# Loading the adjacency of a graph layer in whole 128-partition transfers, from the SP and ScalarE queues

## The reference

```python
# layer 1, on h = layernorm(x)
mask = (adj > 0).astype(x.dtype)             # adj: 4096 x 4096 int32, 64 MiB
deg  = jnp.sum(mask, axis=1, keepdims=True)
agg  = mask @ h / jnp.maximum(deg, 1.0)
self_f, nb_f = h @ W_self + b_self, agg @ W_nb + b_nb
x = x + relu(concatenate([self_f, nb_f], -1) @ W_comb + b_comb)
# layer 2, on h = layernorm(x)
logits = h @ Wg + bg                         # 8 experts
score, idx = top_k(logits, 2); w = softmax(score)
x = x + sum over the two chosen e of w_e * (gelu(h @ W1[e] + b1[e]) @ W2[e] + b2[e])
```

## Time and profile before

| | |
|---|---|
| median of three runs | 504.6 us (504.56 to 507.19) |
| the profiled execution's own time | 503.99 us |
| its span, first to last instruction | 502.2 us |
| busy: PE, DVE, ACT, POOL | 435.5, 374.2, 261.2, 328.7 us |
| mean granted TensorE clock | 0.951 of full speed |
| moved by DMA | 122.48 MB, mean 244 GB/s |

### The profile page before, as it was taken

The page is one execution under the profiler, slowest core; times in us unless marked ns, Lnnn a source line. Parts: engine busy times, 40 slices in busy tenths (PEclk is TensorE's granted clock), DMA queues, the critical chain, the costliest instruction groups (busy, mean ns, idle before and its releaser), DMA issues.

```text
span 502.2 us, 12812 instructions
## 1 busy us (share of the span) xinstructions
PE 435.5 (87%) x4214; PEld 383.2 (76%) x4214; DVE 374.2 (75%) x1056; ACT 261.2 (52%) x403; POOL 328.7 (65%) x348
## 2 busy tenths in 40 slices
PE   5789999799999979999969998954999999997720
PEld 5578888688888868888848887843799999986610
DVE  2899654467779879797758788766677777779972
ACT  2566773144533534445435454233588888886630
POOL 3398585264665878877738876367777868665560
PEclk9999999999999989999979999995899999999975
DMA  8998799889995999799999997296865565598675
GB/s 216 272 292 251 210 228 284 234 236 279 279 279 159 294 280 281 209 292 302 299 295 267 297 310 228 87 286 214 264 194 175 176 178 178 169 337 339 198 220 167
DMA packets 48688, 122.48 MB, mean 244 GB/s; under 512 B 10601, under 2 KB 19693, under 8 KB 47600
## 3 DMA queue, kind: packets, MB, share of 16 engines
q1 hardware_dynamic: 26736, 64.09, 45.0%
q0 software_dynamic: 16144, 50.49, 33.5%
q10 hardware_dynamic: 5744, 7.08, 5.1%
HBM read 96.52 MB, written 26.93 MB: 246 GB/s over the span
## 4 chain that ended last, share of the span: by engine, by line
DVE 32%; PE 31%; DMA 14%; issue 9%; POOL 8%; ACT 3%; SPq 1%; DVEq 1%; ACTq 0%; POOLq 0%
PE bank L1342 8%; PE bank L1362 8%; DMA wst<-in_L_ffn_W_dram 8%; PE bank L1245 7%; DVE maskT L845 5%; POOL rs L633 3%; PE bank L1329 3%; DVE x_sb L930 2%; DVE xh L928 2%; DMA x_sb<-in_x_dram 2%; DVE w L982 2%; DMA stage<-in_adj_dram 2%; DVE st L934 2%; PE bank L1236 2%; ACT xh L725 2%
## 5 line engine op out<-in xcount | busy, mean ns | idle before, releaser
L1236 PE MATMUL bank<-z_flat,maskT 128*128 128x257 f16 x1024 | 231.3, 277 | 7.7 <-issue 7.6
L1237 PE MATMUL bank<-z_lo,maskT 128*128 128x256 f16 x1024 | 231.2, 276 | 0.0
L1236 PEld LDWEIGHTS bank<-z_flat,maskT 128*128 128x128 fp8e4 x1024 | 101.5, 99 | 21.6 <-issue 8.2
L651 POOL DMA_INDIRECT pair_out<-rows,enum x78 | 87.6, 1123 | 39.5 <-issue 18.3
L1237 PEld LDWEIGHTS bank<-z_lo,maskT 128*128 128x128 fp8e4 x1024 | 101.4, 99 | 12.8
L676 ACT ACTIVATE mask<-stage,m 128x2048 fp8e4<-128x2048 int32 x32 | 64.1, 2002 | 53.4 <-DMA stage<-in_adj_dram,gidx 39.7
L584 POOL DMA_INDIRECT dispatched<-rows,slot x64 | 66.4, 1038 | 28.0 <-issue 18.5
L573 POOL DMA_INDIRECT stage<-in_adj_dram,gidx x64 | 67.5, 1054 | 24.9 <-issue 13.3
L725 ACT ACTIVATE xh<-x_sb,nb,rs 128x256 f32<-128x256 f32 x32 | 19.2, 600 | 102.6 <-POOL nb L635 80.4
L633 POOL TENSOR_TENSOR rs<-ve,mhalf 128x1 f32<-128x1 f32 x32 | 39.8, 1245 | 49.4 <-DVE ve L939 49.1
L1342 PE MATMUL bank<-stage,w 128*128 128x256 f16 x468 | 59.7, 279 | 5.6 <-DVE stage L1115 5.3
(11 more groups left out here) (179 smaller groups left out, 604.9 us busy)
## 6 DMA issues: line engine op xcount, KB each, us to landing
stage<-in_adj_dram SPq DMA_DIRECT2D x256, 128.0 KB
stage<-dispatched SPq DMA_DIRECT2D x39, 260.0 KB, 3.0
wst<-in_L_ffn_W_dram ACTq DMA_DIRECT2D x16, 256.0 KB, 10.2
z_lo<-pair_out SPq DMA_DIRECT2D x4, 1024.0 KB, 7.1
dispatched<-pad SPq DMA_DIRECT2D x15, 260.0 KB
out_dram<-x_sb SPq DMA_DIRECT2D x28, 128.0 KB, 4.8
maskT<-pair_out SPq DMA_DIRECT2D x3, 1024.0 KB, 9.6
x_sb<-in_x_dram ACTq DMA_DIRECT2D x6, 256.0 KB, 11.4
```

The costliest lines, as they stand in the source:

```text
L651: gp.indirect_dma_start(out=yp_dram[:, :], out_offset=bass.IndirectOffsetOnAxis(ap=enum[:, a, s:s + 1], axis=0), in_=ysb[:, a, s, :], in_o ...
L1236: mm(acc[u % 2][:, 0:D + 1], a, z_hi[:, i, :], start=(i == 0), stop=False)
L1237: last = mm(acc[u % 2][:, 0:D], a, z_lo[:, i, :], start=False, stop=(i == NT - 1))
```

## The change

The view `adj_q`, the index column `gidx` with its semaphore and the function `gather` go, and with them all of GpSimd's 64 indirect DMAs on the adjacency. SP loads VectorE's half with one transfer for each b, over all 128 partitions, with g and r both taken whole from `adj_v`. For steps 0 and 1 SP loads ScalarE's half too. From step 2 on, ScalarE's own queue issues its half of step t+2 directly behind the mask of step t, after a wait for that mask's semaphore. The semaphore count of VectorE's half falls from 128 to 32 for each fill.

```diff
-    adj_q = adj.rearrange("n (g j) -> (n g) j", g=G)
@@ load_adj on SP
                 for b in range(2):
-                    for g in (0, 2, 1, 3):
-                        sp.dma_start(stage[Q * g:Q * g + Q, s, b, :], adj_v[t // B, t % B, g, :, b, :]).then_inc(s_adj[s], 16)
+                    sp.dma_start(stage[:, s, b, :], adj_v[t // B, t % B, :, :, b, :]).then_inc(s_adj[s], 16)
+                if t < 2:
+                    for b in range(2):
+                        sp.dma_start(stage[:, s + 1, b, :], adj_v[t // B, t % B, :, :, 2 + b, :]).then_inc(s_adj[s + 1], 16)
@@ GpSimd
-            pool.wait_ge(s_pad, 2)
-            for g in range(G):
-                if g:
-                    pool.wait_ge(s_gi, g)
-                gp.iota(gidx[Q * g:Q * g + Q, :], [[0, 1]], base=g, channel_multiplier=4 * B).then_inc(s_gi, 1)
-            pool.wait_ge(s_gi, G)
-            def gather(t):
...
-                if k == 1:
-                    gather(0)
...
-                if k in (2, 4, 5, 7):
-                    gather((2, 4, 5, 7).index(k) + 1)
-            gather(5)
...
-                m = made_in(s)
-                if m is not None and m + 2 < NT:
-                    gather(m + 2)
@@ masks on ScalarE
                 sc.activation(mask[:, u % 2, 2:4, :], stage[:, s], ACT.Sigmoid, bias=m100[:, 0:1], scale=200.0,
                               saturate=False).then_inc(s_mA, 1)
+                if t + 2 < NT:
+                    act.wait_ge(s_mA, t + 1)
+                    for b in range(2):
+                        act.dma_start(stage[:, s, b, :], adj_v[(t + 2) // B, (t + 2) % B, :, :, 2 + b, :]).then_inc(s_adj[s], 16)
@@ masks on VectorE
-                dve.wait_ge(s_adj[s], 128 * (div(t, u, known, 0, 2) + 1))
+                dve.wait_ge(s_adj[s], 32 * (div(t, u, known, 0, 2) + 1))
```

More of the change, by code:

```diff
@@ L114, in gnn_moe_kernel @@
         bcol = sb("bcol", [P, 2, KT], F32)
-        gidx = sb("gidx", [P, 1], I32)
         mhalf = sb("mhalf", [P, B], F32)
@@ L271, in gnn_moe_kernel @@
             "weights_transposed", "wT_copied", "weights_folded", "fold_hi", "fold_scales"))
-        s_gi = sem("gather_indices")
         s_fmx, s_fmr, s_fch, s_wf, s_bb, s_cp, s_cb = (sem(n) for n in (
@@ L614, in _ @@
                         normalise(t)
-                if k in (2, 4, 5, 7):
-                    gather((2, 4, 5, 7).index(k) + 1)
-            gather(5)
             pool.dma_start(b1c[:, :, :], b1.rearrange("e (t p) -> p e t", p=P), allow_slow_non_contiguous=True).then_inc(s_b12, 16)
-            self_and_const(0)
-            gather(6)
-            self_and_const(1)
+            for k in range(2):
+                self_and_const(k)
             LAST_POWERS = NT + X1
```

## The result

The changed kernel takes 904.33 us (median of four runs, 901.41 to 904.65) beside 505.25 us for the kernel before on the same chip: a ratio of 1.787, with an interval of 1.781 to 1.793. The forecast was 915 us. The profiled execution took 901.41 us, its span is 899.2 us.

A forecast was written before the change was run, and what follows sets the result against it. Transfers and TensorE were taken as close bounds before; after the change, four DMA engines. Adjacency 663, other traffic 52, start 2, tail 188 and 2 around the span sum to 907 us; some 8 for gaps gives 915, range 860 to 1130.

The forecast's parts named there:

- The layout: Adjacency transfers: source's outermost count of 4 puts both queues on the same 4 engines, not 16; chance 0.84.
- The rate of one engine: Adjacency transfers: each of four engines moves 25.3 GB/s, not 17.6, so 16.78 MB takes 663 us.
- The rest of the traffic and the gaps: Other transfers on the same engines 52 us, 2 us before them, some 8 us for gaps at the start.
- the queues stay full: Neighbour sum: each engine keeps its queue full, a step taking 21 us plus its share of the rest.
- Behind the last landing: After the last adjacency transfer: 3.2 us, 14.4 us of matmuls at half clock, 170.1 us to the end, together 188 us.
- Cover of ScalarE's issues: ScalarE's queue: 60 issues at 0.465 us, 0.93 us a step, 28 us in all, hidden and taken as 0.
- 300 each: Sign of being right: VectorE's and ScalarE's masks wait for the adjacency for 300 us and more each.
- the 40 us I allowed: Expert weights queue behind up to two steps of ScalarE's half, some 40 us, and just fit.
- GpSimd: Neighbour sum: 64 gathers, 67.5 us busy, go; worth between 0 and 14.6 us if transfers keep pace.
- My rival: Adjacency transfers spread over 16 engines after all, GpSimd's relief gives 0 to 14.6 us: 490 to 504 us; chance 0.12.
- Partition span and number of engines: Adjacency transfers: the 128-partition rule alone would make the change a gain; the outermost-count rule gives 4 engines.

The follow-up runs named there:

- e1: The changed kernel with the source's two outer indices exchanged (r, 32, outermost, then g), so another adjacency is summed: 508.87 us, 0.975 of the kernel before.
- e2: The changed kernel with each adjacency transfer cut into two of 64 partitions, 256 KB each: 1562.48 us, run once.
- e4: The kernel before with only SP's half in whole 128-partition transfers, the gathers kept: 709.97 us, 1.359 of the kernel before.
- e9: The same kernel as e1, run again beside e8 on one chip: 488.6 us, 0.970 of the kernel before.
- e3: The changed kernel with each transfer as four quarters of 32 partitions, 128 KB, on both queues, no gathers: 546.24 us, 1.042 of the kernel before.
- e5: As e3, quarters of 32 partitions on both queues, but both b in one transfer of 256 KB: 523.48 us, 1.036 of the kernel before.
- e8: The kernel before with b = 1 moved from SP's quarters to a third GpSimd gather over 128 partitions: 510.78 us, 1.014 of the kernel before.
- e6: The kernel before with SP's half in quarters of 256 KB, both b in one transfer, gathers kept: 509.0 us, 1.008 of the kernel before.

## Why the prediction was right, point by point

**The layout.** Right, and shown. Four engines carry the adjacency of both queues: 104 GB/s at a share of 0.26 with four packets in flight, e1 with only the index order changed at 0.975, e2 at half the rate with half the count, e4 with one queue alone at the same 104 GB/s.

**The rate of one engine.** I took 25.3 GB/s, from a stretch of long 128-partition loads, over the 17.6 of the sum. Measured: 26.0, on four engines and on two. The adjacency alone is then 16.78 MB / 26.0 = 645 us where I had 663. The choice of 25.3 was an argument, that sixteen engines share a limit which four don't reach, and at 17.6 the forecast would have been 1197 us; e2, with half as many engines and the same 26.0 for each, bears the argument out.

**The rest of the traffic and the gaps.** The last transfer lands at 708.3 us, where I had 663 + 52 + 2 and some 8 for gaps, 725. With 645 us for the adjacency 63 us are left for the rest, the start and any gaps, against my 62. That the queues stay full was right: between 25 and 700 us at least four packets are in flight for over 99% of the time. ScalarE made its 6th mask at 145.05 us and its last at 708.34: 563.3 us for 26 steps, 21.7 us each, where I had 21 us plus its share of the rest.

**Behind the last landing.** 899.2 - 708.3 = 190.9 us, forecast 188, with the right size by two errors. I let one step of matmuls follow, at half clock, 3.2 + 14.4 us. There are two, at nearly full clock: the matmuls of L1213 end at about 730.0, 21.7 us after the landing. ScalarE has the last mask, which waits for the landing, in its order ahead of the normalisation of an earlier tile (L701, L704). VectorE's subtraction L891 waits for that, and TensorE's transposes of the tile (L1258) wait for L891 and stand ahead of the last but one step of matmuls. So the wait for the landing holds two steps, not one. The clock was 0.71 in the mean of the sum, 0.81 to 1.00 in the last two steps, and not near the 0.50 I had taken. What follows is 899.2 - 730.0 = 169.2 us, forecast 170.1.

**Cover of ScalarE's issues.** Priced at 0.93 us a step and hidden. The price was wrong and the conclusion held only because transfers bound everything: two issues of expert weights held ScalarE for 19.11 us, and its L701 waited 244.9 us behind such issues. With the same transfers on 16 engines (e1) the same line is short:

```profile
L670 ACTq DMA_DIRECT2D wst<-in_L_ffn_W_dram x16: 373/438/957, 73.8 to 288.3; - x16
```

And in e4, where the slow transfers are on SP's queue alone, SP's issues reach 12.0 us and ScalarE's no more than 1.3. So an issue is long where the transfers ahead of it in its queue are slow to drain. I read that as a full queue; no view shows how full one is. That is also why the waits for the adjacency are 254.2 and 61.4 us and not 300 each: the engines stood behind one another (L891's 292.7 us), and not only at the landing. The expert weights landed after 20.0 us in the median and 32.1 at most, under the 40 us I allowed, but they didn't quite fit: VectorE waited for them four times, 19.0 us in all.

**GpSimd.** 67.5 us of gathers went and were worth nothing here. In e1 and e9, where the engines are 16, everything the change removes together with its 128-partition form gave 2.5 to 3%, 15.5 us on e9's chip. My rival had put that at 0 to 14.6 us.

**Partition span and number of engines.** e1 is 0.975 and e3 1.042 of the kernel before on one chip: transfers over 128 partitions, with the fewer issues that come with them, are worth 7% if they run on 16 engines, and the changed kernel shows what they cost on four. The Trainium skill's advice to use one 128-partition transfer (DMA: Bandwidth & Descriptors, "Rules for kernel authors"), given there for two halves that both run on all 16 engines, agrees with the first number; for the changed kernel, where the whole transfer runs on four, it doesn't hold. Its rule on the number of engines (same page, "Why a DMA increments its semaphore by 16 and not by 1") agrees with all three counts run here, 32, 4 and 2.

## What to carry to other kernels

Before merging partial loads into one 128-partition transfer, write both patterns down and look at the outermost count of each after all merging: with a 4 there, 12 of 16 DMA engines stand idle, and a share of 0.26 with a flat rate in the profile is what it looks like. When a transfer has to be cut, cut until the small outer index is gone: halves with a count of 2 were slower still (1562 us), quarters with 32 rows outermost were not (546 us). A slow queue can also hold the engine that issues on it, so an engine with other work in its order should not feed one.

## What the runs showed of the hardware that was not expected

- With two or four engines in use each gives 26.0 GB/s on rows of 4 KB (52/2 and 104/4; by share, 104/16/0.26, it is 25.0). With all 16, and all other transfers counted too, each busy engine gave 15.6 to 16.5 GB/s where the adjacency came wholly in transfers of 32 partitions (e5, e3), 17.4 in the kernel before with half of it in gathers over 128 (270/16/0.97 in 75 to 298 us), 20.1 with three quarters (e8) and 21.8 with all of it over 128 (e1). Packets of 4 KB show the same: 161 ns in the median on four engines, 159 in e1, 231 to 233 in the kernel before, 247 in e3 and 264 to 268 in e5. Doubling the size of the quarters didn't help (e5, e6). e1 also reads the memory in another order, the four quarters of a row behind one another; e8 doesn't, and its rate rose all the same. Why 32 partitions are slow is open.
- Issuing on a slow queue blocks the issuer: up to 12.6 us for one issue on SP and 14.9 us on ScalarE, against at most 1.6 us (L455) and 1.0 us (L670) for the same lines on 16 engines in e1.
